# A fused state-space scan and ternary MLP on one core: the last four MLP tiles in an order written out per engine

## What is computed

```python
def mixer(h, z):                       # h = ctx_1024, z = layernorm(x)
    u  = silu(causal_conv4(h @ in_w) + conv_b)          # [b, 512, L]
    dt_low, B, C = split(u @ x_proj_w)                   # 16, 16, 16
    dt = softplus(dt_low @ dt_w + dt_b)
    state = state * exp(dt * A) + (dt * u) * B           # along L, 16 states per channel
    y  = (sum_n state * C + D * u) * silu(z)
    return swapaxes(y, 1, 2)

def bitlinear(x, w):                   # rows quantized to 8 bits, weights to -1, 0, 1
    return act_quant(rmsnorm(x)) @ weight_quant(w).T

x = x + tanh(g_xattn) * mixer(ctx_1024, layernorm(x))
n = layernorm(x)
h = silu(bitlinear(n, w1)) * bitlinear(n, w2)            # [rows, 2048]
x = x + tanh(g_ffn) * bitlinear(h, w3)
```

## Time and profile before

| what | value |
|---|---|
| median of 3 runs | 740.64 us (740.63 to 741.85) |
| the profiled execution's own time | 740.08 us |
| its span in the profile | 738.3 us |
| what lies around the span | 1.78 us |
| busy: DVE, POOL | 605.7 us (82%), 622.7 us (84%) |
| busy: PE, ACT | 521.0 us (71%), 522.6 us (71%) |
| mean granted clock of TensorE | 0.881 of 2.4 GHz |

### The profile page before, as it was taken

The page is one execution under the profiler, slowest core; times in us unless marked ns, Lnnn a source line. Parts: engine busy times, 40 slices in busy tenths (PEclk is TensorE's granted clock), DMA queues, the critical chain, the costliest instruction groups (busy, mean ns, idle before and its releaser), DMA issues.

```text
span 738.3 us, 8115 instructions
## 1 busy us (share of the span) xinstructions
PE 521.0 (71%) x2562; PEld 317.3 (43%) x2562; DVE 605.7 (82%) x834; ACT 522.6 (71%) x984; POOL 622.7 (84%) x297
## 2 busy tenths in 40 slices
PE   9778988475444668777748586777767867776785
PEld 3244434134332435454535354444545545444342
DVE  7679778978998989788779889998988898985451
ACT  5844766179767768876877878897898976753751
POOL 1599899889999999999999999899988999880011
PEclk9899999788566989989768899999999999999797
DMA  4695866069920000255200000275200000000000
GB/s 164 248 400 202 295 249 251 28 256 382 414 92 6 28 2 15 85 189 199 99 20 29 0 15 0 69 236 209 72 1 14 2 15 14 1 15 15 1 14 28
DMA packets 23929, 80.77 MB, mean 109 GB/s; under 512 B 2432, under 2 KB 4608, under 8 KB 20816
## 3 DMA queue, kind: packets, MB, share of 16 engines
q1 hardware_dynamic: 23888, 80.27, 29.9%
HBM read 72.53 MB, written 7.73 MB: 109 GB/s over the span
## 4 chain that ended last, share of the span: by engine, by line
DVE 29%; PE 23%; ACT 22%; POOL 11%; issue 11%; DMA 3%; SPq 1%; POOLq 0%; DVEq 0%; ACTq 0%
DVE hh L739 8%; ACT da L709 5%; POOL hh L687 4%; POOL hh L758 4%; DVE hh L736 4%; PE bank_t L1048 4%; PE bank_t L1031 3%; PE bank_y L788 3%; PE bank_a L935 3%; ACT room L1038 3%; PE bank_b L941 2%; DMA wq<-x 2%; ACT room L953 2%; DVE sm L641 2%; ACT room L974 2%
## 5 line engine op out<-in xcount | busy, mean ns | idle before, releaser
L739 DVE TENSOR_TENSOR_SCAN hh<-da,hh 128x1024 f32<-128x1024 f32 x96 | 217.6, 2277 | 6.9 <-POOL hh L687 3.5
L788 PE MATMUL bank_y<-ident,hh 128*128 128x128 f32 x1024 | 148.0, 294 | 22.5 <-POOL hh L758 18.0
L758 POOL TENSOR_TENSOR hh<-hh,cc 128x1024 f32<-128x1024 f32 x64 | 160.7, 2510 | 2.4 <-DVE hh L739 2.4
L788 PEld LDWEIGHTS bank_y<-ident,hh 128*128 128x128 f32 x1024 | 131.7, 154 | 53.0 <-POOL hh L758 25.2
L753 POOL TENSOR_TENSOR hh<-hh,cc 128x1024 f32<-128x1024 f32 x64 | 150.7, 2356 | 3.0 <-ACT hl L722 1.9
L687 POOL TENSOR_TENSOR hh<-pair,bb 128x1024 f32<-128x1024 f32 x30 | 71.7, 2393 | 24.9 <-DMA bb<-xd_scratch 24.7
L736 DVE TENSOR_TENSOR_SCAN hh<-da,hl,hh 128x256 f32<-128x256 f32 x128 | 85.1, 729 | 0.0
L681 POOL TENSOR_TENSOR hh<-wq,bb 128x1024 f32<-128x1024 f32 x32 | 75.4, 2355 | 7.2 <-PE bank_y L788 7.2
L687 POOL TENSOR_TENSOR hh<-wq,bb 128x1024 f32<-128x1024 f32 x32 | 76.8, 2400 | 3.9 <-PE bank_y L788 3.9
L681 POOL TENSOR_TENSOR hh<-pair,bb 128x1024 f32<-128x1024 f32 x32 | 75.3, 2353 | 3.3 <-PE bank_y L788 3.3
L1038 ACT ACTIVATE room<-bank_t,sm 128x512 bf16<-128x512 f32 x60 | 41.0, 684 | 45.0 <-PE bank_t L1031 45.0
(11 more groups left out here) (237 smaller groups left out, 1040.6 us busy)
## 6 DMA issues: line engine op xcount, KB each, us to landing
bb<-xd_scratch SPq DMA_DIRECT2D x32, 512.0 KB, 5.2
cc<-xd_scratch SPq DMA_DIRECT2D x32, 512.0 KB, 7.1
wq<-weights SPq DMA_DIRECT2D x12, 1024.0 KB, 5.5
stage<-weights SPq DMA_DIRECT2D x8, 1024.0 KB, 6.3
xin<-x SPq DMA_DIRECT2D x4, 1024.0 KB, 5.2
room<-weights SPq DMA_DIRECT2D x4, 1024.0 KB, 8.2
u_scratch<-wq SPq DMA_DIRECT2D x6, 512.0 KB, 3.5
wq<-x SPq DMA_DIRECT2D x2, 1024.0 KB, 18.0
```

The source lines that it names most:

```text
L739: ins = v.tensor_tensor_scan(h, flat(dbank[k % 2]), h, 0.0, ALU.mult, ALU.add)
L758: ins = g_.tensor_tensor(hh[k % NH][:, :, :], hh[k % NH][:, :, :], cc[:, s * GN:(s + 1) * GN, :], ALU.mult)
L788: mm = pe.matmul(bank_y[:, (first + c) * P:(first + c + 1) * P], flat(hh[k % NH])[:, at:at + P], ident[:, :], start=False, stop=(s == STEP ...
```

## The change

- `END` is 13: tile 13 too uses silu, the additional banks and rounding on POOL.
- The slot loops end after slot 124. All that comes later (the last scan itself still stands in the loop) is a list of calls per engine, 37 of them on PE.
- On PE `sums(124)` to `sums(127)` stand ahead of chunks 1 to 3 of tile 13, and pieces of the tiles are interleaved: the transposes of one tile between the chunks of the next.
- The squares of tiles 13 to 15 are three instructions in place of four (chunks 0 and 1 as one of 1024 columns, `square_end`), written to scan buffers that are free; the peaks likewise (`peak_end`). The tanh or silu buffer is free as soon as h is formed.
- DVE copies out some of the transposed chunks: two each of tiles 12, 14 and 15 (`hqt_vector`, `by_vector`).
- The second half of tile 12's rounding goes to POOL. The last tile's h is rounded in four pieces, two on ACT and two on POOL (`hq_last`), and its four transposes go to four different banks. `out_tensor` waits for each group of four blocks by itself; the last one takes the groups in the order 0, 2, 1, 3.
- `fin` has two copies, so that `scales_vector` of a tile needs not wait for `out_vector` of the tile before.
- The loops over the tiles on ACT, PE and DVE are cut in two, since they have different ends now. On ACT and PE no instruction before the lists changes its place. On DVE `z_vector` now stands ahead of the other loop, so that in the ten slots where both occur it comes before `peak_vector` and `out_vector` and no longer after.

```diff
-END = 14
+
+END = 13
+SLOTS = ALL - LEAD + 1
...
         def bank_x(i):
-            return bank_y if at_end(i) else bank_t
+            return bank_y if i > END else bank_t
 
         def bank_h(i, g):
-            return dbank[1][:, 0, :] if at_end(i) and g % 2 else bank_t
+            if i == NB * NE - 1:
+                return (bank_t, bank_y, dbank[1][:, 0, :], dbank[0][:, 0, :])[g]
+            return dbank[1][:, 0, :] if i >= END - 1 and g % 2 else bank_t
...
+            if i == END and c == 1:
+                pe.wait_ge(s_scan, ALL - 1)
+                before = (-1, 0)
+            elif at_end(i):
...
+        def square_end(act, i, c):
+            act.wait_ge(*MV.of(("h", i, c)))
+            if i > END:
+                act.wait_ge(*MA.of(("sq", i - 1, c)))
+            else:
+                act.wait_ge(s_sum, ALL - LEAD)
...
+        def hq_last(eng, line, i, c):
+            eng.wait_ge(*MV.of(("csh", i)))
+            h = h_at(i)[:, c, :]
...
+        def by_vector(i, g):
+
+            return MV if i in (12, 14, 15) and g >= 2 else MA
...
+        def hqt_vector(v, i, g):
+            v.wait_ge(*MP.of(("hT", i, g)))
+            v.wait_ge(*MP.of(("o", i - 1)))
+            MV.did(v.tensor_scalar(hqT[:, 4 * g:4 * g + 4, :].rearrange("p a b -> p (a b)"), bank_h(i, g)[:, :],
+                                   -MAGIC, None, ALU.add), ("hqT", i, g))
...
+            for g in groups:
+                if i >= END - 1:
+                    pe.wait_ge(*by_vector(i, g).of(("hqT", i, g)))
...
@@ -1335,7 +1452,7 @@
-                for k in range(LAST):
+                for k in range(SLOTS):
...
+                sums(pe, 124)
+                sums(pe, 125)
+                ab_tensor(pe, 13, 1)
...
+                out_tensor(pe, 15, (0, 2, 1, 3))
...
                     for i in TILES:
-                        u = tile_slot(i)
-                        if at_end(i) and k == (u - 1 if i == END else u - 2):
-                            rows_vector(v, i, 1)
                         if k == z_slot(i):
                             z_vector(v, i)
                         if i < NE and k == z_turn_slot(i):
                             y_first(v, i)
+                    for i in range(END):
+                        u = tile_slot(i)
                         if k == u + 2:
                             peak_vector(v, i, 0)
                         if k == u + 4:
                             peak_vector(v, i, 1)
-                        if k == u + 6 and at_end(i):
-                            scales_vector(v, i, 1)
                         if k == turned(i) + 2:
                             out_vector(v, i)
```

More of the change, by code:

```diff
@@ L1146, in _ @@
                 load_x_rows(0, 3)
-                for k in range(0, LAST + 2):
+                for k in range(SLOTS):
                     for b in (1, 2, 3):
@@ L1301, in _ @@
                             square_scalar(act, i, c)
-                        if k == u + 7 and not at_end(i):
+                        if k == u + 7:
                             hq_scalar(act, i, 0)
```

313 lines of the change are left out of this document (234 added, 79 removed).

## The result

The changed kernel takes 717.77 us (median of 4 runs, 716.77 to 717.98), beside 740.71 us for the kernel before on the same chip: ratio 0.9684, 95% interval 0.9667 to 0.9701. The profiled execution took 717.76 us with a span of 716.0. The forecast was 717.3 us. That it is so near is luck to a large part: one of its terms was 4.5 us too small, another 4.3 us too large.

The account below looks back on a forecast made before the run. PE's work was taken to bound the end: sums(124) at 658.8, plus 45.3 work, 3.8 waits and 4.3 clock put the last out_vector at 712.2, 22.8 us earlier, hence 717.3 us from 740.08. Range 710.8 to 724.5.

Parts of the forecast that it names:

- What bounds the end: From sums(124) on, PE has the most work of all engines, 45.3 us, the least this end can take.
- The waits PE keeps: In the end PE still waits 1.6 for sums(127), 1.1 for row tile 14, 0.8 for a bank, 0.3 in small ones.
- The last rounding "just arrives in time": Tile 15's chain from last silu to rounding, 4.5 us, fits within 5.8 us of PE's other work.
- the margin of 1.3 us: Slack at tile 15 between its rounding chain and PE's other work, put at only about 1.3 us.
- What the change costs ahead of the lists: Moving z_vector ahead in ten slots delays sums(124) by 1.8 us, to 658.8; the earlier nine slots cost nothing.
- the 4 us at which the text called itself wrong: Sign of a wrong forecast: sums(124) late by over 4 us, meaning the exchange of z_vector cost more.
- the 1.8 for slot 116: DVE idles before z in slot 116, then does output (0.66) and peak (1.12): a 1.8 us shift, bounds 0 and 2.65.
- 3.6 more if the cover is gone: If POOL's late reading of scans stops hiding the exchange in two more slots, 3.6 us come on top.
- The clock: PE's granted clock in the end taken as 0.92, as in the stretch from 617 to 659, adding 4.3 us.
- The sum: 658.8 + 45.3 + 3.8 = 707.9, with 4.3 for the clock 712.2 for the last out_vector, 22.8 us earlier.
- The rivals: Open hand-overs between tiles, 723.9 (chance 0.20); full clock without shift, 711.2 (0.13); clock low throughout, 758.3 (0.02).
- Full clock and no shift: Rival: slot 116's shift is swallowed and PE stays at 2.4 GHz in the end, 711.2 us, chance 0.13.

Follow-up runs that it names:

- e4: Changed kernel with out_vector of tile 14 on DVE put back ahead of the last scales of tile 15: 723.31 us, ratio 0.9737.
- e10: Kernel of e4 with PE multiplying constants into a free bank during its wait before the transposes of tile 15: 721.21 us, ratio 0.9716.
- e2: Kernel before the change with only z_vector moved ahead of peak and output in the ten slots: 744.85 us, ratio 1.0047.
- e1: Changed kernel with z_vector put back behind peak_vector and out_vector in all ten slots: 713.49 us, ratio 0.9611.
- e12: Kernel of e1 measured a second time beside the kernel before the change: 713.12 us, ratio 0.9597.
- e7: Kernel of e1 with all six copies of transposed chunks moved from DVE back to ACT: 713.41 us, ratio 0.9627.
- e8: Kernel of e1 with tile 15 rounded by POOL in two instructions and the last product's groups in order 0 to 3: 715.39 us, ratio 0.9651.
- e11: Kernel of e1 with the transposes of tile 13 behind all chunks of tile 14, ACT reordered to match: 714.11 us, ratio 0.9619.
- e9: Kernel of e1 with PE's slot loop also placing the next tile's chunk between two groups of transposes: 720.1 us, ratio 0.9699.
- e3: Changed kernel with sums(125) to sums(127) on PE put back one by one between tile 13's chunks: 726.16 us, ratio 0.9781.
- e5: Changed kernel with z_vector put back behind peak and output in slot 116 alone: 716.65 us, ratio 0.9671.
- e6: Changed kernel with z_vector behind out_vector but still ahead of peak_vector in the ten slots: 716.25 us, ratio 0.9658.

## Why the prediction came out right, and where it did not

- **What bounds the end.** Right. PE's 45.3 us of work were measured as 45.36 busy, and its work plus 2.9 us of waits is the whole end.
- **The waits PE keeps.** `sums(127)` 1.47 for 1.6; row tile 14 0.99 for 1.1. The 0.8 for a bank of tile 14 was half there (0.43). Sum 2.9 for 3.8.
- **The last rounding "just arrives in time".** It does: PE goes from tile 14's product to the transposes of tile 15 with no wait worth a row. e4 shows how thin that cover is, as the margin of 1.3 us said: with the output back in front PE waits 2.62 us, and pays 1.2 more for the clock.
- **What the change costs ahead of the lists.** Wrong: `sums(124)` at 663.27, not 658.8, which is over the 4 us at which the text called itself wrong. The step that failed is that the earlier nine slots cost nothing because POOL reads a scan at least 3.2 us after it ended, and with it the 1.8 for slot 116. The scan is not the only thing that POOL takes from this chain. It takes `bank_y` back from PE's sums, which PE can start only when DVE has gated the group (behind slots 86 and 110, 1.1 each, of which 0.5 and 0.4 are matmuls at the low clock), and the scale for its power from DVE (slot 116, 2.02), and there sums again, behind PE's wait for the output (0.78). I named the `sums` behind PE's wait and did not follow it to POOL, though my own rows showed POOL waiting 10.5 us for such sums. Two such slots were my "3.6 more if the cover is gone", priced but not taken; 2.2 came. The total of the exchanges is 5.5 us in place of 1.8, with some 0.6 of drift on top.
- **The clock.** Wrong by the whole term: 1.00, not 0.92, so 4.3 us too many. The stretch of 617 to 659 was no model, since PE waits there again and again, up to 2.9 us, and is busy 77% of it, where it was 93% in the new end. The end after 663 has two pauses of 1.5 and 1.0 us and no other over 0.5. The first of the two rules that I weighed, of the Trainium skill, page "TensorE: Matmul & The Clock Gate", section "What's actually happening" (idleness brings the low level, sustained work keeps the high one), agrees with this trace and with e10, though not with every pause: after 4.01 us in e2 the groups ran at the full clock. With it and the true shift the sum is 663.3 + 45.3 + 3.8 = 712.4 for the last `out_vector`, which came at 711.54.
- **The sum.** 4.5 us too little for the shift, 4.3 too much for the clock, 0.9 too much for waits; the last `out_vector` came at 711.54, forecast 712.2. That the first two cancel is luck: nothing ties them to each other. The part behind it was 1.2 us longer than in the profile of before (3.7 against 2.5 from its end to the span's end), though its code is the same; e1 shows 3.0, e12 3.7.
- **The rivals.** None took place as a whole. "Full clock and no shift" had the clock right. Its 711.2 is what the version with z put back nearly gives: its profiled executions took 712.5 (e1) and 711.9 (e12).

Open: why the drift ahead of the lists differs between executions of one order (0.1 to 3.2 us at step 127 over five profiles with the same order there: e1, e7, e8, e11, e12). The low-clock stretches do not lie at the same places in all of them, and POOL's waits for sums move with them, but no run fixed them. The low stretch behind the gate of slot 86 is in all six profiles with z ahead of both and in no other, so it belongs to the exchange; for that behind slot 110 this is not shown, since e9, with z back, has it too. The tanh form of tile 13, its extra banks, and the three squares for four were not undone alone.

## What to carry to other kernels

Before an instruction is moved ahead on an engine that is not the bottleneck, list everything that the bottleneck engine takes from this engine, directly and over a third one: results, freed buffers, small scalars. Lag on one of them (the scans' 3.2 us) covers only that one. Where several engines have work left at the end, filling the waits of the one with the most work can pay twice, once for the wait and once for the clock behind it, as undoing it cost twice in e3 and e4. A move that pays where its source engine is idle (the lists) can cost where that engine is full (e9).

## What the runs showed of the hardware

- After PE pauses of 1.98 (e3), 2.62 (e4) and 3.93 us (e3) the next groups ran at 1.2 GHz, at once or after one group (transposes about 0.9 apart in place of 0.46; w1 and w2 groups 1.91 long in place of 1.03; the w3 product 4.93 in place of 3.62). After pauses of 1.47 and 0.99 us in a dense stretch there was no change over 48 us. A pause makes the low level likely, not certain: that of 4.01 us in e2 was followed by groups at full clock, the same pause before the change (4.02) by groups at the low one. Matmuls of constants in the 2.6 us pause kept 2.4 GHz (e10); six passes of 128x512 in float32 took 2.74 us.
- Copies of 128x512 from PSUM with conversion to bfloat16 took 0.68 us each on DVE (L1097), nearly the same as on ACT (0.69, L1091).
- One order of instructions gave starts of `sums(124)` from 657.1 to 660.2 us over five profiles, so a difference of 1 us in the time of one execution says nothing here, while the length of the stretch from `sums(124)` to the last product repeats within 0.01 us (44.61 us after, 44.62 in e1, e5, e6 and e12).
